# Recurrent layers: where the chosen state part is turned to features

## The chip, the cores and the metric

The kernel runs on one core of a Trainium2 chip, as one program. The metric is the device time of one launch in microseconds (us). The engines named here are TensorE (PE in the profile, with its weight loads as PEld), VectorE (DVE), ScalarE (ACT), GpSimd (POOL) and the sync engine (SP), which issues the weight loads from HBM.

## The reference, cut to what matters

Four layers run over 4 samples of 512 tokens and 512 features: an attention with shared keys, a decoder layer with two attentions and an MLP, and two recurrent layers (`L2` and `L3`). The change lies in the recurrent layers only. What they compute there, for 32 heads of 16 features each:

```
r, k, v = xr @ Wr.T, xk @ Wk.T, xv @ Wv.T            # 32 heads of 16
w = exp(-exp(decay + tanh(xw @ td_w1) @ td_w2))
def step(s, (r_t, k_t, v_t, w_t)):
    a = k_t[..., :, None] * v_t[..., None, :]
    out = einsum('bhi,bhij->bhj', r_t, u * a + s)
    return a + w_t[..., :, None] * s, out
og = (out - mean) / sqrt(var + 1e-5)                 # mean and var over the 16 of a head
x1 = x + (og * gn_w + gn_b) * g @ Wo.T
```

## The kernel before, in words

One loop (`nc.Fori`) goes over the 4 samples; a sample passes through all four layers before the next one begins. Each engine has its own instruction stream, written out by hand; semaphores join them. There is no planner: the order of the calls in the source is the order on the engine.

The features of a recurrent layer are split into `C = 4` groups of 128 (8 heads), counted by `hg`. The scan over tokens is not done step by step. Tokens are cut into blocks of 8. Inside a block, the outputs come from sums over pairs of tokens at distances that double (`pair_sums` of level 0, 1, 2 and `pair_sums4`, `bonus_low`, `bonus_high`), and these are built up in one bank of PSUM in feature-by-token layout, `y_bank`. What a token takes from the state with which its block began comes by another way. `fresh_state` makes each block's new state (128 matmuls of 32x32), DVE scans the states over the blocks (`states`), and `from_state` multiplies them with `r` (128 matmuls of 32x32) into the banks 0 to 3 of PSUM. Each of those holds four candidates, of which ACT and DVE choose one for every token by a mask: ACT in one instruction (`y_tokens`, line 1416), DVE in three (`own_block`, line 1250). The result is `y_tok`, in token-by-feature layout. `tokens_to_y` (line 990 to 994) turns it to features with 16 small products against the identity, which show as 32 matmuls in the trace, and adds it to `y_bank`. After that, ACT takes the bank out twice (`y_out`: its square to `sqT`, a copy to `yT`), and PE makes the variance of each head (`variance`).

`middle(hg, n)` gives PE other work in between: the projection of `k`, `r` or `v` for the next group (line 369, eight matmuls of 128x512 in the trace), and in the last group the gate in their place. `values_to_tokens` (line 909) turns `v` to tokens; it waits for ACT's copy `vT` (line 1375), and ACT's `value_blocks` (line 1432) spreads its result. `keys_to_tokens` (line 953) does the same for `k`, and ACT's copy of it is `k_tok` (line 1451), for which `fresh_state` waits. `pair_sums(hg, 0)` writes into bank 0, so for `hg > 0` it waits until DVE is done with `y_tok` of the group before (line 915). ACT's own order in a group is: `value_blocks`, (in the last group a copy of a weight block, line 324), `middle(hg, 0)`, `y_out(hg - 1)`, `k_tok`, then the rest.

The weights come in blocks of 1 MB into a ring of three places, `wring` (line 278). SP issues the next block as soon as the last product with the oldest one is done. In the recurrent groups that falls after the last projection of `k`, of `r` and of `v`, all in the group `hg = 2`.

The three places between two groups are called the first (`hg` 0 to 1), the middle (1 to 2) and the third transition (2 to 3). There are 8 of each: 2 layers in 4 samples.

Of the kernel before, what the change touches and what calls it, by code (L numbers as in the profile page):

```python
# [21 lines left out]
C = H // P  # L22
# [73 lines left out]
def build(nc, a, known, samples=B):  # L96
# [116 lines left out]
    with ExitStack() as stack:  # L213
# [97 lines left out]
        def w_parts(name):  # L311
            buf, k = SPLIT[name]
            return buf[:, k % 2, 0, :], buf[:, k % 2, 1, :]
# [17 lines left out]
        def parts_wait(pe, name):  # L331
            pe.wait_ge(*act_done.when('whi', name))
            pe.wait_ge(*low_made(name))
# [6 lines left out]
        def three(w, src):  # L340

            return ((w[0], src[0]), (w[1], src[0]), (w[0], src[1]))
# [486 lines left out]
        def pe_rwkv(pe, l):  # L829
# [31 lines left out]
            def project(hg, name, fcs=range(C)):  # L861
                if hg == 0 and 0 in fcs:
                    w_wait(pe, f'{name}_{l}')
                tile = take(pe, f'{name}p', l, hg) if hg > 0 else ps[:, FIRST[name], :]
                to_T(pe, tile, weights(f'{name}_{l}'), mix[:, MIX_AT[name]], hg, fcs=fcs,
                     fin=tile_ready.reach(f'{name}p', l, hg) if C - 1 in fcs else None,
                     ready=(lambda fc: mix_wait(pe, l, name, fc)) if hg == 0 else None)
# [31 lines left out]
            def gate(c):  # L899
                if c == 0:  # L900
                    w_wait(pe, f'g_{l}')
                to_T(pe, take(pe, 'gp', l, c), weights(f'g_{l}'), mix[:, MIX_AT['g']], c, fin=tile_ready.reach('gp', l, c),
                     ready=(lambda fc: mix_wait(pe, l, 'g', fc)) if c == 0 else None)

            def values_to_tokens(hg):
                pe.wait_ge(*act_emptied.when('vp', l, hg))
                tile = take(pe, 'vt', l, hg)
                for tc in range(C):
                    m = nc.tensor.matmul(tile[:, tc * P:(tc + 1) * P], vT[:, hg % 2, tc * P:(tc + 1) * P], centre[:, :],
                                         start=True, stop=True)  # L910
                m.then_inc(*tile_ready.reach('vt', l, hg))

            def pair_sums(hg, level):
                if level == 0 and hg > 0:
                    pe.wait_ge(*dve_done.when('y_tok', l, hg - 1, 3))
                pe.wait_ge(*dve_done.when('rk', l, hg, level))
                bank, src = ((0, rk0[:, :]), (1, rk1[:, :]), (2, rk2[:, :, :, :]))[level]
                nc.tensor.matmul(ps[:, bank, 0:256 if level == 1 else 512], head_sum[:, :], src, start=True, stop=True)\  # L918
                    .then_inc(*tile_ready.reach('sums', l, hg, level))

            def pair_sums4(hg):
                pe.wait_ge(*dve_done.when('rk', l, hg, 4))
                for part in range(2):
                    nc.tensor.matmul(take(pe, 'sums4', l, hg, part), head_sum[:, :], rk4[:, 2 * part:2 * part + 2, :, :],  # L924
                                     start=True, stop=True).then_inc(*tile_ready.reach('sums4', l, hg, part))
# [23 lines left out]
            def keys_to_tokens(hg):  # L949
                pe.wait_ge(*dve_done.when('k8', l, hg))  # L950
                tile = take(pe, 'kt', l, hg)
                for tc in range(C):
                    m = nc.tensor.transpose(tile[:, tc * P:(tc + 1) * P], kT[:, hg % 2, tc * P:(tc + 1) * P], ident[:, :])
                m.then_inc(*tile_ready.reach('kt', l, hg))

            def fresh_state(hg):
                for level in range(3):
                    pe.wait_ge(*dve_emptied.when('sums', l, hg, level))
                pe.wait_ge(*act_emptied.when('vt', l, hg))
                pe.wait_ge(*act_emptied.when('kt', l, hg))  # L960
                for tc in range(C):
                    for r in range(4):
                        rows_ = slice(32 * r, 32 * r + 32)
                        for q in range(4):
                            out = ps[32 * q:32 * q + 32, r, :].rearrange('p (two t x) -> p two t x', two=2, t=C)[:, :, tc, :]
                            m = nc.tensor.matmul(out, k_tok[rows_, tc, 32 * q:32 * q + 32],
                                                 v_blocks[rows_, tc, q, :, :, :].rearrange('p two b j -> p two (b j)'),
                                                 start=True, stop=True)
                m.then_inc(*S['fresh_ready'].reach(l, hg))
# [19 lines left out]
            def tokens_to_y(hg):  # L989
                pe.wait_ge(*dve_done.when('y_tok', l, hg, 3))  # L990
                for tc in range(C):
                    for p in range(4):
                        m = nc.tensor.matmul(y_bank[32 * p:32 * p + 32, tc * P:(tc + 1) * P], y_tok[:, p, tc, :], ident[:, :],
                                             start=False, stop=(tc == C - 1), skip_group_check=True)
                m.then_inc(*S['context_ready'].reach('y', l, hg))

            def variance(hg):
                pe.wait_ge(*act_done.when('sqT', l, hg))
                tile = take(pe, 'var', l, hg)
                for tc in range(C):  # L1000
                    m = nc.tensor.matmul(tile[:, tc * HEADS:(tc + 1) * HEADS], sqT[:, tc * P:(tc + 1) * P],
                                         masks[:, 4:4 + HEADS], start=True, stop=True)
                m.then_inc(*tile_ready.reach('var', l, hg))

            def roots_to_features(hg):
                pe.wait_ge(*(dve_done if hg == C - 1 else pool_done).when('rstd_j', l, hg))
                tile = take(pe, 'rs', l, hg)
                for tc in range(C):
                    m = nc.tensor.transpose(tile[:, tc * P:(tc + 1) * P],
                                            rstd_j[:, tc, :, :].rearrange('p h j -> p (h j)'), ident[:, :])  # L1010
                m.then_inc(*tile_ready.reach('rs', l, hg))

            def wo(fc, tiles=range(C)):
                if fc == 0 and 0 in tiles:
                    parts_wait(pe, f'o_{l}')
                    pe.wait_ge(*dve_done.when('y_tok', l, C - 1, 3))
                pe.wait_ge(*dve_done.when('gated_lo', l, fc))
                for tc in tiles:
                    for k, (w, x_) in enumerate(three(w_parts(f'o_{l}'), (act_hi[:, 2], act_lo[:, 2]))):
                        m = nc.tensor.matmul(ps[:, tc, :], x_[:, fc, tc * P:(tc + 1) * P], w[:, fc * H:(fc + 1) * H],  # L1020
                                             start=(fc == 0 and k == 0), stop=(fc == C - 1 and k == 2), skip_group_check=True)
                    if fc == C - 1:
                        m.then_inc(*tile_ready.reach('wo', l, tc))

            def middle(hg, n):
                if hg + 1 < C:
                    project(hg + 1, 'krv'[n])
                else:
                    gate(n)

            for hg in range(C):
                values_to_tokens(hg)
                pair_sums(hg, 0)
                pair_sums(hg, 1)
                middle(hg, 0)
                if hg > 0:
                    tokens_to_y(hg - 1)
                pair_sums(hg, 2)
                keys_to_tokens(hg)
                if hg > 0:  # L1040
                    variance(hg - 1)
                fresh_state(hg)
                pair_sums4(hg)
                bonus_low(hg)
                middle(hg, 1)
                if hg == C - 1:
                    gate(C - 1)
                if hg > 0:
                    roots_to_features(hg - 1)
                bonus_high(hg)  # L1050
                from_state(hg)
                middle(hg, 2)
            wo(0, (0, 1))
            tokens_to_y(C - 1)
            wo(0, (2, 3))
# [524 lines left out]
        with nc.Fori(0, samples) as b:  # L1580
# [8 lines left out]
            with nc.Block() as block:  # L1589
                @block.tensor  # L1590
                def _(pe):
# [32 lines left out]
                    for l in (2, 3):  # L1624
                        pe_rwkv(pe, l)
# [276 lines left out]
```

## Time and profile before

| what | us |
|---|---|
| median of 3 runs | 4186.95 |
| lowest and highest | 4186.92, 4193.72 |
| profiled execution, its own time | 4188.31 |
| its span | 4186.5 |
| PE busy | 3719.4 (89%) |
| DVE busy | 2621.0 (63%) |
| ACT busy | 2154.2 (51%) |
| POOL busy | 1652.4 (39%) |

The span reaches from the first to the last instruction that was profiled. A time in a row of the trace counts from the span's start. Busy times of engines overlap, so they don't add up to the span. The mean granted clock of TensorE in the profiled execution is 0.952 of full speed.

### The profile page before, as it was taken

What the parts mean: (1) busy time and instruction counts of PE and PEld (TensorE: products, weight loads), DVE (VectorE), ACT (ScalarE), POOL (GpSimd) and SP (SyncE); (2) the same over time, 40 slices, a digit from 0 to 9 for tenths busy, and PEclk for the clock granted to TensorE, in tenths of its full rate; (3) what the DMA queues carried; (4) which work ended last, traced back from release to release, by engine and by line L of the source; (5) the groups of instructions that cost most, each with busy time, mean ns of one, the idle gap of its engine ahead of it and who ended that gap; (6) DMA issues with size and microseconds to landing.
All of it is one profiled execution on the core that took longest, in us unless ns stands there. A gap on an engine that the chain in (4) does not pass through costs nothing. (4 is left out here: it accounts for less than half of the span.)

```text
span 4186.5 us, 66406 instructions
## 1 busy us (share of the span) xinstructions
PE 3719.4 (89%) x24448; PEld 2267.5 (54%) x24448; DVE 2621.0 (63%) x5691; ACT 2154.2 (51%) x4272; POOL 1652.4 (39%) x1849
## 2 busy tenths in 40 slices
PE   7988899899888989989888888998988888899898
PEld 4544565546554456554655445656465454565555
DVE  5765746666576564665657656467666765645766
ACT  5655733434666573343466657334346665733433
POOL 4554442232454454223245445422324544542232
PEclk9999999999999999999999999999999999999999
DMA  4032221102204122110220412211022032221102
GB/s 137 15 103 67 78 78 40 62 21 101 76 15 123 49 84 70 39 64 21 101 76 15 121 53 82 70 42 60 22 101 78 20 117 55 78 70 42 60 32 101
DMA packets 94558, 276.11 MB, mean 66 GB/s; under 512 B 25472, under 2 KB 25984, under 8 KB 73088
## 3 DMA queue, kind: packets, MB, share of 16 engines
q1 hardware_dynamic: 94208, 271.58, 20.2%
q8 instruction: 202, 3.31, 0.3%
q14 instruction: 148, 1.21, 0.1%
HBM read 201.24 MB, written 4.19 MB: 49 GB/s over the span
## 5 line engine op out<-in xcount | busy, mean ns | idle before, releaser
L805 POOL TENSOR_SCALAR probs<-probs,row_inv 128x512 f32<-128x512 f32 x1024 | 696.0, 696 | 635.1 <-DVE row_inv L720 635.1
L664 ACT ACTIVATE probs<-probs,row_max 128x512 f32<-128x512 f32 x1024 | 733.4, 725 | 132.1 <-DVE row_max L736 131.2
L559 PE MATMUL ps<-ident,probs 128*128 128x128 f32 x4096 | 606.5, 289 | 172.9 <-ACT pT L658 146.5
L559 PEld LDWEIGHTS ps<-ident,probs 128*128 128x128 f32 x4096 | 477.0, 146 | 383.0 <-ACT pT L658 211.4
L658 ACT ACTIVATE pT<-ps 128x512 f32<-128x512 f32 x768 | 430.1, 602 | 107.2 <-PE ps L559 106.5
L369 PE MATMUL ps<-mix,wring 128*128 128x512 f32 x1024 | 471.0, 596 | 3.8 <-DMA wring<-in_blocks_dram 3.8
L534 PE MATMUL ps<-kstack,qstack 96*128 96x512 f32 (+1 forms) x1024 | 380.5, 467 | 16.2 <-DMA qstack<-hi 7.1
L736 DVE CUSTOM_DVE_ANT_0 probs<-ps,maskA 128x512 f32<-128x512 f32 x512 | 329.3, 681 | 42.6 <-PE ps L534 42.6
L736 DVE CUSTOM_DVE_ANT_0 probs<-ps,neg 128x512 f32<-128x512 f32 x512 | 340.6, 685 | 8.9
L369 PEld LDWEIGHTS ps<-mix,wring 128*128 128x128 f32 x1024 | 191.2, 190 | 198.9 <-issue 178.8
L1535 POOL TENSOR_TENSOR hinv<-hvar,minus_half 128x32 f32<-128x32 f32 x24 | 146.3, 6094 | 376.8 <-DVE hvar L1255 376.8
L550 PE MATMUL ps<-pT,v 128*32 128x512 f32 x2048 | 244.6, 599 | 0.0
L369 PE MATMUL ps<-srcT,wring 128*128 128x512 f32 x512 | 238.5, 609 | 0.2
L534 PEld LDWEIGHTS ps<-kstack,qstack 96*128 96x128 f32 (+1 forms) x1024 | 177.1, 194 | 108.4 <-issue 44.1
L409 POOL TENSOR_SCALAR varep<-moments 128x1 f32<-128x1 f32 x128 | 43.0, 336 | 482.1 <-DVE moments L388 481.1
L329 POOL TENSOR_TENSOR mlp_w<-wring,mlp_w 128x2048 fp32r<-128x2048 f32 x32 | 149.5, 4672 | 194.2 <-ACT mlp_w L324 194.2
L421 PE MATMUL ps<-ident,xn 128*128 128x128 f32 x448 | 104.8, 389 | 126.6 <-DVE xn L392 126.1
L750 DVE COPY pT<-ps 128x512 f32<-128x512 f32 x256 | 168.2, 686 | 73.2 <-PE ps L559 71.7
L664 ACT ACTIVATION_READ_ACCUMULATOR probs<-probs,row_max 128x1 f32 x1024 | 205.4, 201 | 0.0
L1689 DVE TENSOR_TENSOR hidden_lo<-hidden,hidden_hi 128x512 fp32r<-128x512 f32 x64 | 94.2, 1495 | 168.7 <-ACT hidden_hi L1656 168.7
L1510 POOL TENSOR_TENSOR mix<-mix,xa 128x512 f32<-128x512 f32 x104 | 118.6, 1160 | 171.6 <-DVE mix L1126 122.4
L743 DVE TENSOR_TENSOR ps<-ps,maskA 128x1024 f32<-128x1024 f32 x128 | 156.5, 1223 | 23.1 <-PE ps L534 22.9
(177 smaller groups left out, 7025.9 us busy)
## 6 DMA issues: line engine op xcount, KB each, us to landing
wring<-in_blocks_dram SPq DMA_DIRECT2D x151, 1024.0 KB, 5.1
qstack<-hi SPq DMA_DIRECT2D x256, 64.0 KB, 2.0
kstack<-hi SPq DMA_DIRECT2D x256, 64.0 KB, 2.0
maskA<-in_mask_dram SPq DMA_DIRECT2D x9, 1024.0 KB, 7.8
rows<-in_rows_dram SPq DMA_DIRECT2D x8, 1024.0 KB, 4.6
qstack<-hi SPq DMA_DIRECT2D x256, 32.0 KB, 2.0
qstack<-lo SPq DMA_DIRECT2D x128, 64.0 KB, 2.0
kstack<-lo SPq DMA_DIRECT2D x128, 64.0 KB, 2.0
```

What stands on the lines that cost most here:

```text
L329: nc.gpsimd.tensor_tensor(low, weights(name), high.bitcast(F32), ALU.subtract).then_inc(*pool_done.reach('wlo', name))
L369: m = nc.tensor.matmul(tile, w[:, base_ + fc * H + oc * P:base_ + fc * H + (oc + 1) * P], src[:, fc, :], start=(fc == 0), stop=(fc == C - 1))
L534: nc.tensor.matmul(ps[:, qc, :], qstack[0:A.kt, g % 2, i, qc * P:(qc + 1) * P], kstack[0:A.kt, g % 2, 0 if A.shared else i, :], start=True ...
L550: ins = nc.tensor.matmul(ps[32 * h:32 * h + 32, OBANK, :], lhs, pT[:, h, kc, :], start=(kc == 0 and first), stop=(kc == C - 1 and final))
L559: ins = nc.tensor.transpose(tile[:, qc * P:(qc + 1) * P], probs[:, m % PSLOTS, qc, kc * P:(kc + 1) * P], ident[:, :])
L658: nc.scalar.activation(pT[:, m % 4, kc, :], ps[:, ring.bank('pT', t, m, kc), :], ACT.Copy)\
L664: nc.scalar.activation(p, p, ACT.Exp, bias=row_max[:, n % PSLOTS, qc:qc + 1], scale=-1.0, accum_out=row_sum[:, n % PSLOTS, qc:qc + 1]).the ...
L736: nc.vector.tensor_tensor_reduce(out=probs[:, s, qc, :], in0=ps[:, qc, :], in1=other, scale=-1.0, scalar=3.0e38, op0=ALU.add, op1=ALU.min, ...
L743: nc.vector.tensor_tensor(ps[:, two, :], ps[:, two, :], A.mask[:, two, :], ALU.mult)\
L750: nc.vector.tensor_copy(pT[:, m % 4, kc, :], ps[:, ring.bank('pT', t, m, kc), :])\
L805: nc.gpsimd.tensor_scalar(p, p, row_inv[:, (n - 1) % PSLOTS, qc:qc + 1], 1.0, ALU.mult, ALU.mult)\
L1535: nc.gpsimd.tensor_tensor(hinv[:, :, :], hvar[:, :, :], minus_half[:, :].rearrange('p (a b) -> p a b', b=HEADS), ALU.pow).then_inc(*pool_d ...
```

## The change: the step is moved by one place

PE's list of calls changes, and nothing else: the function, its waits, and the streams of the other engines stay as they are. `tokens_to_y(hg - 1)` stood in group `hg` behind the projection `middle(hg, 0)`. Now `tokens_to_y(hg)` stands at the end of group `hg`, behind `middle(hg, 2)`, for `hg` 0, 1 and 2. The call for the last group stays where it was, between two parts of `wo`.

```
                 pair_sums(hg, 0)
                 pair_sums(hg, 1)
                 middle(hg, 0)
-                if hg > 0:
-                    tokens_to_y(hg - 1)
                 pair_sums(hg, 2)
                 keys_to_tokens(hg)
                 if hg > 0:
...
                 bonus_high(hg)
                 from_state(hg)
                 middle(hg, 2)
+                if hg < C - 1:
+                    tokens_to_y(hg)
             wo(0, (0, 1))
             tokens_to_y(C - 1)
```

So PE's order across a transition was: `v` projection, `values_to_tokens`, `pair_sums` 0 and 1, `k` projection (or the gate), `tokens_to_y`, `pair_sums` 2, `keys_to_tokens`, `variance`, `fresh_state`. It becomes: `v` projection, `tokens_to_y`, `values_to_tokens`, `pair_sums` 0 and 1, `k` projection (or the gate), `pair_sums` 2, and on as before.

## Rows read from the trace of the kernel before

**Rows 1.** The profile page, busy time (us, share, instructions) and DMA queues (packets, MB, share).

```profile
PE 3719.4 (89%) x24448; PEld 2267.5 (54%) x24448; DVE 2621.0 (63%) x5691; ACT 2154.2 (51%) x4272; POOL 1652.4 (39%) x1849
...
q8 instruction: 202, 3.31, 0.3%
```

**Rows 2.** Timeline around the middle transition of sample 1, layer 2 (start, duration, instructions).

```profile
696.30 3.70 PE L369 MATMUL ps<-mix,wring 128*128 128x512 f32 x8
...
697.13 2.32 DVE L1250 SCALAR_TENSOR_TENSOR y_tok<-ps,masks,y_tok 128x512 f32<-128x512 f32 x3 [2.64 <-ACT y_tok L1416]
...
700.69 1.16 PE L909 MATMUL ps<-centre,vT 128*128 128x128 f32 x8 [0.69 <-ACT vT L1375]
...
702.97 3.60 PE L369 MATMUL ps<-mix,wring 128*128 128x512 f32 x8
...
706.50 1.08 PE L993 MATMUL ps<-ident,y_tok 128*32 128x128 f32 x32
706.60 0.33 SPq L278 DMA_DIRECT2D wring<-in_blocks_dram  x1
706.61 0.60 ACT L1375 ACTIVATE kT<-ps 128x512 f32<-128x512 f32 x1 [2.30 <-PE ps L369]
707.51 1.12 PE L918 MATMUL ps<-rk,head_sum 128*128 128x512 f32 x2
707.65 0.60 ACT L1423 ACTIVATE sqT<-ps 128x512 f32<-128x512 f32 x1 [0.44 <-PE ps L993]
708.14 0.59 ACT L1424 ACTIVATE yT<-ps 128x512 f32<-128x512 f32 x1
...
709.11 0.60 ACT L1451 ACTIVATE k_tok<-ps 128x512 f32<-128x512 f32 x1 [0.37 <-PE ps L953]
...
709.85 1.72 PE L966 MATMUL ps<-v_blocks,k_tok 32*32 32x128 f32 x108
...
713.50 0.47 PE L966 MATMUL ps<-v_blocks,k_tok 32*32 32x128 f32 x20 [1.93 <-issue]
```

**Rows 3.** Stretches, first transition (window length, each engine's busy time, PEclk, DMA share, GB/s).

```profile
667.43:694.45 27.02, 26.25 (x362) 15.86 (x363) 17.66 (x41) 8.85 (x13) 6.32 (x4) 1.00 0.01 2
```

**Rows 4.** Stretches, middle transition: two of eight, and the sum of eight.

```profile
1738.71:1770.52 31.81, 29.20 (x362) 16.87 (x362) 17.62 (x42) 8.74 (x13) 6.28 (x4) 0.89 0.14 41
...
4052.45:4079.46 27.01, 26.25 (x362) 15.86 (x362) 17.68 (x42) 8.85 (x13) 6.25 (x4) 1.00 0.17 52
sum 242.46, PE 223.61 PEld 131.28 DVE 140.89 ACT 70.56 POOL 50.04; mean PE 27.95 PEld 16.41 DVE 17.61 ACT 8.82 POOL 6.25
```

**Rows 5.** DMA queues, first transition, 675 to 677 us (packets, MB, share).

```profile
q8 instruction: 1, 0.02, 4.2%
```

**Rows 6.** DMA queues, 704 to 710.5 us: the only queue; the issue (us to landing).

```profile
q1 hardware_dynamic: 117, 0.96, 41.7%
...
wring<-in_blocks_dram SPq DMA_DIRECT2D x1, 1024.0 KB, 4.7
```

**Rows 7.** DMA queues, middle transition, 710.5 to 712 us.

```profile
q8 instruction: 1, 0.02, 5.4%
```

**Rows 8.** Timeline around the third transition of sample 1, layer 2.

```profile
737.06 0.59 ACT L1423 ACTIVATE sqT<-ps 128x512 f32<-128x512 f32 x1
...
737.90 0.69 DVE L1211 TENSOR_TENSOR rk<-ps,vT 128x512 f32<-128x512 f32 x1 [2.85 <-PE ps L918]
...
738.26 0.60 ACT L1451 ACTIVATE k_tok<-ps 128x512 f32<-128x512 f32 x1
...
742.35 0.41 PE L966 MATMUL ps<-v_blocks,k_tok 32*32 32x128 f32 x4 [1.49 <-issue]
```

**Rows 9.** Stretches, third transition: two of eight, and the sum of eight.

```profile
723.60:757.49 33.89, 31.71 (x372) 18.07 (x371) 20.57 (x44) 12.49 (x17) 8.05 (x3) 0.95 0.16 57
...
2814.93:2845.24 30.31, 29.62 (x372) 17.33 (x371) 20.76 (x43) 12.49 (x17) 10.17 (x2) 1.00 0.17 64
...
sum 268.19, PE 251.18 PEld 143.70 DVE 164.72 ACT 99.89 POOL 66.44; mean PE 31.40 PEld 17.96 DVE 20.59 ACT 12.49 POOL 8.31
```

More of the change, by code:

```diff
@@ L1035, in pe_rwkv @@
                 middle(hg, 0)
-                if hg > 0:
-                    tokens_to_y(hg - 1)
                 pair_sums(hg, 2)
@@ L1052, in pe_rwkv @@
                 middle(hg, 2)
+                if hg < C - 1:
+                    tokens_to_y(hg)
             wo(0, (0, 1))
```

## The prediction, made before the changed kernel was timed

> **What bounds the kernel now.** First the page: TensorE is busy for 89% of the span [rows 1]. So the question at each transition between two groups is what PE does and where it stands idle, and the views to read are the timeline there and the stretches from one `from_state` to the next. I give places in the middle transition of sample 1, layer 2 [rows 2]; the other 23 look alike where I don't say otherwise.
>
> PE finishes the `v` projection a little before 700.0, stands idle for 0.69 us until ACT's `vT`, starts `values_to_tokens` at 700.69, the `k` projection at 702.97, `tokens_to_y` at 706.50, `pair_sums` 2 at 707.51, and `fresh_state` at 709.82 to 709.85, right behind ACT's `k_tok`, which ends at 709.11 + 0.60 = 709.71. The reader is to see two things there: the idle 0.69 us, while DVE has finished `y_tok` at 697.13 + 2.32 = 699.45; and that `fresh_state` breaks off after 108 of its 128 matmuls and stands still for 1.93 us, for nothing that a semaphore explains ("issue").
>
> Then the stretches. A first transition takes 27.02 us [rows 3]. The eight middle ones take 242.46 us together, 30.3 on average, but the last of them takes 27.01 with the same instructions [rows 4]. So 242.46 - 8 x 27.01 = 26.4 us are lost in seven of them. PE's busy time makes 223.61 - 8 x 26.25 = 13.6 of that: the same matmuls at a lower granted clock (0.89 in the slowest, against 1.00). The other 12.8 are idle time, 1.8 in each of seven. In the third transition seven of eight have such a stop too, with 4 matmuls left [rows 8]: 268.19 - 8 x 30.31 = 25.7 us over the one that has none [rows 9], of which PE's busy time makes 251.18 - 8 x 29.62 = 14.2 and idle time 11.5.
>
> **What the stop is.** Queue 8 moved 202 packets of instructions, 3.31 MB [rows 1]. Over them, PE's 48,896 loads and matmuls make 242 a packet, so this is PE's code, coming in blocks of some 250 instructions. The stops fit the ends of blocks: a group issues 725 loads and matmuls [rows 3] and about ten waits, and the stop of the third transition is 16 matmuls (32 instructions) later in `fresh_state` than that of the middle one; together some 767, three blocks. Count one block back from the middle stop: 216 instructions of `fresh_state`, 16 of `variance`, 8 of `keys_to_tokens`, 4 of `pair_sums` 2 make 244, so the block before ends inside the last few instructions of `tokens_to_y`. When PE's sequencer comes to that point, the next block is asked for. In the first transition, where the point is 32 instructions earlier, its packet runs between 675 and 677 us [rows 5], four us before its own `tokens_to_y`: the sequencer is ahead of the array. In the middle transition no instruction packet runs from 704 to 710.5; SP's load of 1 MB, issued at 706.60 when the `k` projection frees its place, takes 4.7 us to land [rows 6], and the packet comes only behind it, between 710.5 and 712 [rows 7]. `fresh_state` uses up its block at 711.6 and waits until 713.50.
>
> The Trainium skill says, in "Runtime: NRT & Kernel Launch", section "Instruction fetch mechanics", that each engine fetches its code in blocks of 16 KiB, ahead of need, and that the cost of crossing a block is mostly hidden. The trace agrees on the size (3.31 MB over 202 packets) and not on the cost, if my reading of the stops is right. By the page's rule there would be nothing to gain from moving a block's end, and the sum would hold the order alone: that is the first rival below.
>
> **The change, part by part.** It removes and adds no instruction. It moves 64 loads and matmuls and one wait.
>
> (a) *Order on PE.* `tokens_to_y` costs 707.51 - 706.50 = 1.01 us, and 0.09 more for the change of shape before it (the projection's eight slots of 0.43 us from 702.97 end at 706.41), 1.10 in all. In its new place it starts at 699.83 (696.30 + 8 x 0.43 + 0.09), 0.38 after `y_tok` is done, so the wait that it brings costs nothing; queued behind it are only `values_to_tokens` and what follows, and these would have waited for `vT` until 700.69. They now start at 699.83 + 1.01 = 700.84: 0.15 late. So `pair_sums` 2 comes 1.10 - 0.15 = 0.95 earlier. What is late next is ACT: `kT` at 706.61 + 0.15, `sqT` and `yT`, which no longer wait for `tokens_to_y`, and `k_tok` follow at 0.49 each (708.14 - 707.65), so `k_tok` starts at 708.23 in place of 709.11. I take 0.88 us for the first and middle transitions: 16 x 0.88 = 14.1. Bounds: 0 if another chain holds `fresh_state`, 16 x 0.95 = 15.2. The chain behind `fresh_state` (sums, DVE's scan, `pairs`, `from_state`) hangs on it and comes along. In the third transition ACT is the bound already: `sqT` starts at 737.06 with no idle time before it, so it moves 0.15 later, and `k_tok` to 737.06 + 0.15 + 0.98 = 738.19 against 738.26 [rows 8]. I take 8 x 0.07 = 0.6.
>
> SP's queue: the `k` block's load is issued 0.15 later. The wait of `pair_sums(hg, 0)` for `y_tok` is met already. `y_bank` is written 5.7 us earlier; nobody reads or writes it between.
>
> (b) *The middle stop.* The count of instructions up to `fresh_state` is what it was, so the stop's place in `fresh_state` stays. But the block before it now ends in the `k` projection, since the 64 instructions of `tokens_to_y` are no longer between. The sequencer gets there some 4 us earlier than before. The packet then runs between about 701 and 705.5, ahead of the load, whose issue is at 706.75, and the block is there when `fresh_state` needs it at 710.7. I take all of the 26.4. Bounds: 0 and 26.4; the row it is nearest to is the middle transition at 27.01 us [rows 4].
>
> (c) *The third stop.* Here the block before ends in `variance`, behind the moved step, in both orders. I take it that the sequencer is held there by `fresh_state`'s first wait, for DVE's product with `pair_sums` 2, which starts at 737.90 after 2.85 us of waiting [rows 8]. That product comes 0.95 earlier with `pair_sums` 2; `fresh_state` starts only 0.07 earlier. So a stop of 1.5 becomes one of 0.6: 7 x 0.88 = 6.2. What remains is as short as the 0.69 us before `values_to_tokens`, after which the clock doesn't fall; but the clock's answer to it no row shows, and I take half of the 14.2. Bounds: 0 and 25.7. Value: 13.3.
>
> **Sum.** 14.1 + 0.6 + 26.4 + 13.3 = 54.4 us. Against the profiled execution's own 4188.3 (span 4186.5 and 1.8 around it) that gives 4133.9. The median of the runs is 1.4 lower, so I predict 4132.5, rounded to 4133.
>
> **The rivals.**
> 1. *The order alone.* Blocks are not what stops PE, or the block is asked for only when PE itself is at its end. Then, with the end among the last of the `k` projection's instructions (about 706.5), the packet still meets the load of 706.75. For it: in the middle and third transition the packet did come late, and only the first shows it well ahead. Against: that first one, and the transition at 27.01. Time: 4187 - 14.7 = 4172. Chance 0.20.
> 2. *Both stops go.* One third transition in eight has none at 30.31 us, with the same code. If 0.95 us are enough to tip the others: 4187 - 14.7 - 26.4 - 25.7 = 4120. Chance 0.11.
> 3. *Slower: the clock falls at the new seam.* `from_state`, then eight matmuls, then 32 narrow ones with 32 columns of weights: if TensorE's granted clock (2.4 GHz) went to its lower level (1.2 GHz) there in each of the 24 transitions, as it does after the stops, each would pay 29.20 - 26.25 = 2.95 us [rows 4], 70.8 in all, where 13.6 + 14.2 = 27.8 are paid now. With the order's 14.7 and the idle 12.8 gained, that is 15.5 slower: 4202. It decides from about 19 falls on. Against: the same narrow matmuls stand ahead of `fresh_state` now, and the clock is 1.00 in the first transition [rows 3]; and PE gets less idle time, not more. Chance 0.07.
> 4. *Nothing.* `k_tok` or DVE's chain holds `fresh_state` where it is, and the stops stay: 4187. The rows speak against both halves at once. Chance 0.04.
>
> **How the numbers follow.** My forecast has 0.58. Its own range, from (c) at nothing to (c) nearly whole, is 4122 to 4146. Leaving out rivals 3 and 4 and the upper edge of rival 1, the range is 4114 to 4174. A difference of less than 0.2% (8.4 us, so above 4178.6 and below 4195.3) could not be told from none. Faster by more than that: 0.58 + 0.20 + 0.11 = 0.89. Within it: 0.04. Slower: 0.07.
>
> **What would show it right or wrong.** In the new profile: `tokens_to_y` directly behind the `v` projection, with no idle time before `values_to_tokens`; the first transition at 26.1 us; the middle ones at 26.1 too, with all 128 matmuls of `fresh_state` in one piece, a clock of 1.00, and the instruction packet ahead of SP's load. If the middle ones stay near 30, (b) is wrong. The third ones at 30.2 to 33.8 tell of (c): the stop with 4 matmuls left should be about 0.6 us. If `y_tok` is what `tokens_to_y` waits for, (a) is wrong.

## The result and the profile after

The changed kernel takes 4168.6 us (median of 19 runs, 4148.0 to 4193.5), against 4186.9 beside it (19 runs, 4177.2 to 4199.9): a ratio of 0.996, interval (95%) 0.9948 to 0.9972. That is 18 us faster, where 54 were forecast. The profiled execution took 4193.5 (span 4191.6) and so lies at the upper end of its own kernel's runs. Two more executions of the same kernel, profiled later and described under the experiments, are nearer to the median. I show the order of the work from the first and take sizes from all of them.

The page after: the same instructions and the same number of code packets.

```profile
PE 3721.5 (89%) x24448; PEld 2264.1 (54%) x24448; DVE 2621.2 (63%) x5691; ACT 2149.2 (51%) x4272; POOL 1650.0 (39%) x1849
...
q8 instruction: 202, 3.31, 0.3%
```

The timeline around the middle transition of sample 1, layer 2, which answers to [rows 2] (start, duration, instructions):

```profile
703.14 3.70 PE L369 MATMUL ps<-mix,wring 128*128 128x512 f32 x8
...
703.97 2.32 DVE L1250 SCALAR_TENSOR_TENSOR y_tok<-ps,masks,y_tok 128x512 f32<-128x512 f32 x3 [3.37 <-ACT y_tok L1416]
...
706.77 1.08 PE L993 MATMUL ps<-ident,y_tok 128*32 128x128 f32 x32
...
706.88 0.60 ACT L1375 ACTIVATE vT<-ps 128x512 f32<-128x512 f32 x1 [2.94 <-PE ps L369]
...
707.78 1.16 PE L909 MATMUL ps<-centre,vT 128*128 128x128 f32 x8
...
710.07 3.60 PE L369 MATMUL ps<-mix,wring 128*128 128x512 f32 x8
...
713.50 1.02 PE L918 MATMUL ps<-rk,head_sum 128*128 128x512 f32 x2
713.70 0.33 SPq L278 DMA_DIRECT2D wring<-in_blocks_dram  x1
...
715.15 0.62 ACT L1451 ACTIVATE k_tok<-ps 128x512 f32<-128x512 f32 x1
...
715.91 1.89 PE L966 MATMUL ps<-v_blocks,k_tok 32*32 32x128 f32 x128
```

`tokens_to_y` (L993) stands behind the `v` projection, `values_to_tokens` (L909) follows with no idle time, and here `fresh_state` (L966) runs its 128 matmuls in one piece. But in sample 2 the same transition has a stop, with 20 matmuls left as in [rows 2], and longer: 2.71 us, where it was 1.93.

```profile
1750.65 0.33 SPq L278 DMA_DIRECT2D wring<-in_blocks_dram  x1
...
1752.87 1.73 PE L966 MATMUL ps<-v_blocks,k_tok 32*32 32x128 f32 x108
...
1757.30 0.70 PE L966 MATMUL ps<-v_blocks,k_tok 32*32 32x128 f32 x20 [2.71 <-issue]
```

And the first transition, which never had a stop before [rows 3], has one in three of eight. This is sample 1:

```profile
684.58 1.44 PE L966 MATMUL ps<-v_blocks,k_tok 32*32 32x128 f32 x92
687.86 1.29 PE L966 MATMUL ps<-v_blocks,k_tok 32*32 32x128 f32 x36 [1.84 <-issue]
```

The stretches from one `from_state` to the next (window, length, each engine's busy time, granted clock, DMA share, GB/s) show what such a stop costs. The first two rows and the first sum are first transitions, the next two and their sum middle ones, the last three third ones:

```profile
669.96:701.31 31.35, 29.47 (x362) 17.19 (x363) 17.57 (x41) 8.52 (x13) 6.34 (x4) 0.89 0.01 2
...
891.67:917.89 26.22, 26.14 (x362) 15.97 (x363) 17.63 (x41) 8.63 (x13) 6.32 (x4) 1.00 0.01 2
...
sum 222.73, PE 216.38 PEld 130.22 DVE 140.88 ACT 68.86 POOL 50.62; mean PE 27.05 PEld 16.28 DVE 17.61 ACT 8.61 POOL 6.33
...
701.31:727.48 26.17, 26.15 (x363) 15.92 (x362) 17.60 (x41) 8.63 (x13) 6.21 (x3) 1.00 0.16 53
...
1738.24:1769.92 31.68, 28.92 (x363) 16.98 (x363) 17.63 (x42) 8.53 (x13) 6.28 (x4) 0.89 0.13 43
...
sum 240.67, PE 224.15 PEld 132.91 DVE 140.92 ACT 68.64 POOL 49.93; mean PE 28.02 PEld 16.61 DVE 17.62 ACT 8.58 POOL 6.24
...
727.48:757.83 30.35, 29.62 (x370) 17.49 (x370) 20.78 (x44) 12.37 (x17) 10.23 (x3) 1.00 0.17 62
...
1769.92:1801.80 31.88, 31.18 (x371) 18.11 (x371) 20.89 (x43) 12.38 (x17) 8.13 (x2) 0.95 0.16 59
...
sum 267.61, PE 254.68 PEld 146.18 DVE 165.00 ACT 99.03 POOL 66.53; mean PE 31.84 PEld 18.27 DVE 20.62 ACT 12.38 POOL 8.32
```

An undisturbed transition is as long as was worked out: 26.2 for 27.0. What was not foreseen is how many are disturbed. With a stop, the two disturbed ones shown take 5.1 and 5.5 us more (31.35 - 26.22, 31.68 - 26.17), idle time and lower clock together; over the nine of this trace it is 3.8 to 6.1. The three sums make 731.0 us, against 726.8 in the trace of before (middle 242.5 [rows 4], third 268.2 [rows 9], and the eight first transitions below), and all the rest of the span is the same (3460.6 and 3459.7). So the whole difference between these two traces lies in the 24 stretches.

```profile
sum 216.12, PE 209.97 PEld 126.87 DVE 141.22 ACT 70.81 POOL 50.41; mean PE 26.25 PEld 15.86 DVE 17.65 ACT 8.85 POOL 6.30
```

### The profile page after: what moved, and what is told of

It reads as the page before. It is cut to its first block and busy times, and to the rows that moved or that the text cites. A ratio compares the mean times of both kernels' runs of the same rounds, so it can differ in the third digit from the quotient of the medians.

```text
span 4191.6 us, 66406 instructions
## 1 busy us (share of the span) xinstructions
PE 3721.5 (89%) x24448; PEld 2264.1 (54%) x24448; DVE 2621.2 (63%) x5691; ACT 2149.2 (51%) x4272; POOL 1650.0 (39%) x1849
```

## The experiments

The question was why the stops did not go. Three ideas: the stops are late blocks of PE's code, and what decides is on which instruction a block ends; they come from SP's load running in front of the packet; or they belong to `fresh_state`, whatever the blocks do. The direct test is to move the ends of all blocks and nothing else.

**Blocks moved by 72 instructions, in both kernels.** Ahead of layer 2's recurrent part PE gets 18 small products whose result is overwritten before anything reads it. Each makes two loads and two matmuls, so all that follows in that sample's layers 2 and 3 lies 72 instructions further on in its block:

```
     def pe_rwkv(pe, l):
+        if l == 2:
+            for _ in range(18):
+                nc.tensor.matmul(ps[0:32, OBANK, 0:8], ident[0:32, 0:32],
+                                 masks[0:32, 0:8], start=True, stop=True)
         pe_norm_turn(pe, f'a{l}', xn2)
```

> The changed kernel with 18 small products of 32x32 (72 loads and matmuls) put into PE's stream once per sample, ahead of the first recurrent layer; nothing else differs, so every later instruction of the recurrent layers lies 72 instructions later against the ends of the code blocks. Theory 1 (the stops are late code blocks, and only the place of a block's end decides): in layer 2 the ends fall at instruction 112, 145 and 177 of fresh_state in the three later groups, with the end before them at least 79 instructions ahead of fresh_state. No stop is left: first and middle transitions 26.1 to 26.2 us, third 30.2 us, clock 1.00 in all, total 4123 us. Theory 2 (the stops belong to the code or to the weight load, wherever the block ends): stops stay after 104 to 124 matmuls, total about 4169 us.

> The kernel before with the same 72 added loads and matmuls. Theory 1: no stops; first and middle transitions 27.0 us, third 30.3, total 4136 us. The difference from the changed kernel with the same addition is then the order alone: 8 x (0.88 + 0.88 + 0.07) = 14.7 us. Theory 2: stops stay, 4187 us.

Measured: the changed kernel 4137.0 (5 runs, 4131.7 to 4139.2), ratio 0.988 (0.9862 to 0.9898); the kernel before 4147.6 (5 runs, 4143.2 to 4149.0), ratio 0.9906 (0.9889 to 0.9923); the kernel before beside them 4188.4 (23 runs). `fresh_state` runs in one piece in all of the 48 transitions. The sums, with the products in the changed kernel (first, middle, two third transitions, third):

```profile
sum 214.54, PE 210.82 PEld 128.55 DVE 140.90 ACT 69.04 POOL 50.28; mean PE 26.35 PEld 16.07 DVE 17.61 ACT 8.63 POOL 6.29
...
sum 209.64, PE 209.17 PEld 127.77 DVE 141.17 ACT 69.03 POOL 49.98; mean PE 26.15 PEld 15.97 DVE 17.65 ACT 8.63 POOL 6.25
...
722.40:754.41 32.01, 31.28 (x370) 18.14 (x370) 20.93 (x44) 12.37 (x17) 8.01 (x3) 0.95 0.15 59
...
942.44:972.79 30.35, 29.62 (x370) 17.49 (x370) 20.77 (x43) 12.37 (x17) 10.20 (x2) 1.00 0.17 62
...
sum 247.84, PE 241.99 PEld 141.81 DVE 166.97 ACT 98.95 POOL 73.06; mean PE 30.25 PEld 17.73 DVE 20.87 ACT 12.37 POOL 9.13
```

and in the kernel before (first, middle, third):

```profile
sum 221.15, PE 211.79 PEld 127.63 DVE 141.13 ACT 70.77 POOL 50.30; mean PE 26.47 PEld 15.95 DVE 17.64 ACT 8.85 POOL 6.29
...
sum 216.03, PE 210.01 PEld 126.89 DVE 141.32 ACT 70.76 POOL 49.91; mean PE 26.25 PEld 15.86 DVE 17.67 ACT 8.85 POOL 6.24
...
sum 242.64, PE 236.89 PEld 139.04 DVE 166.31 ACT 99.86 POOL 81.62; mean PE 29.61 PEld 17.38 DVE 20.79 ACT 12.48 POOL 10.20
```

What follows: added work makes both kernels faster, by 41 us (before) and 32 (changed). The stops hang on the place of the blocks, and `fresh_state` and SP's load alone don't make them. The order is worth 216.03 - 209.64 = 6.4 us in eight middle transitions, 0.80 each. It has a price that I hadn't seen: in the new order three third transitions took 32.0 at a clock of 0.95 with no stop at all, in the old order all eight took 30.3.

Both kernels stayed 12 to 14 us above the times that were expected. In either of them four of the eight first transitions, all in layer 3, have a stop of another kind: PE stands still for 0.5 to 1.1 us inside the `v` projection that opens them, where the addition has put the end of another block. The clock stays whole after it, but first transitions take 221.2 in the kernel before for 216.1, and outside the 24 stretches it has 8 us more than without the addition.

**SP's load put behind the `r` projection,** to take it away from the middle packet. The `k` block's place in the weight ring is given back one projection later, so that two loads run together after `r`; computed is the same.

```
-    f'k_{l}': ('kp', l, 3),
+    f'k_{l}': ('rp', l, 3),
```

> The kernel before, but SP issues the load that follows the last k projection only after the last r projection, some 15 us later (one entry of the table of last uses). Theory A (the 1 MB load holds back the code block in the middle transition): the middle transitions come to 27.0 us, the third ones stay at 33.9, total 4161 us. Theory B (the block is late by itself, the load only lies behind it): the middle stops stay, total 4187 us.

> The changed kernel with the same later load. Theory A: the middle transitions, of which six in eight have a stop of 2.7 us with the packet right behind the load, come to 26.2 us; first ones keep their occasional stop; total about 4140 us. Theory B: the packet comes about 1 us after fresh_state begins, as in the first transition, and the stop shrinks from 2.7 to at most 1.9 us; total 4160 us.

Measured: before with the late load 4177.3 (12 runs, 4162.3 to 4192.0), ratio 0.9983 (0.9966 to 1.0); changed with the late load 4181.0 (12 runs, 4177.3 to 4197.0), 0.9987 (0.9973 to 1.0). In the kernel before, four of seven middle stops go (middle sum 228.6 for 242.5). They are layer 2's; layer 3 keeps the three that it had. Here is one of these, sample 2, layer 3 (timeline of PE), and the one code packet of PE from 1977 to 1979 us, when no other queue moves anything:

```profile
1976.21 1.71 PE L966 MATMUL ps<-v_blocks,k_tok 32*32 32x128 f32 x106
1979.83 0.48 PE L966 MATMUL ps<-v_blocks,k_tok 32*32 32x128 f32 x22 [1.91 <-issue]
```

```profile
q8 instruction: 1, 0.02, 3.7%
```

From 1970 to 1977 queue 8 is silent. So the packet begins 1.0 us after `fresh_state`, with no load in its way, and a stop of 1.91 follows. In the changed kernel the first transitions, which have no load either, keep three stops; the middle ones have four; the third ones get worse, with eight of eight disturbed and a sum of 277.2. What follows: a load isn't needed for a late packet. It changes how late they are, and in the kernel before perhaps how many (three for seven, by one trace each; in the changed kernel four, where its three traces with the load have six, two and one): with the load of the changed kernel, issued 2.2 us ahead of `fresh_state`, the late packet comes about 2.1 us after `fresh_state` begins and the stop is 2.7 us; without it, 1.0 and 1.9. That is also what makes the middle stop of [rows 2] and the one of 2.71 differ: in the kernel before the load is issued 3.2 us ahead, and the packets begin 0.4 to 1.6 after. None of the four expected totals came: 4177 lies between 4161 and 4187, and 4181 above both 4140 and 4160, for the third transitions got worse.

**Blocks moved by 232, by 32, by 64, and the third transition in its old order.** The next four ask three things: can a stop be put into the first transition of the old order, where there never was one (58 products ahead of `pe_norm_turn`, 232 instructions); how near must a block's end lie (8 products, 32 instructions); and what does the new order do in the third transition by itself. For that, `tokens_to_y` of the last pair of groups stays where it was:

```
     middle(hg, 0)
+    if hg == C - 1:
+        tokens_to_y(hg - 1)
     pair_sums(hg, 2)
...
     middle(hg, 2)
-    if hg < C - 1:
+    if hg < C - 2:
         tokens_to_y(hg)
```

This stands in two kernels, with `range(18)` and `range(16)` for the added products.

> The kernel before with 58 added products (232 loads and matmuls): the blocks' ends move 24 instructions the other way. In layer 2 they lie 48 instructions ahead of fresh_state in the first transition, 15 in the middle one, and in the third one inside fresh_state at 17, with none behind it there. Theory 1 (place decides): the stops change their transition. Third ones have none, 30.3 us in all eight; middle ones behave like the third ones of before (a stop of about 1.5 us near the end of fresh_state in most, 29 to 31 us); first ones, which never had a stop in this order, get some (27.0 to 31 us). Theory 2 (the stop belongs to the transition): first 27.0, middle 30.3, third 33.9 us as before.

> The changed kernel with 8 added products (32 loads and matmuls). Block ends lie 104, 71 and 39 instructions ahead of fresh_state in the first, middle and third transition of layer 2, 5 more in layer 3. Theory 1: every place behaves as it did in the transition where it lay before. First: no stop, 26.2. Middle (71, now with the weight load behind it): mostly no stop, as in the first transition of the changed kernel, some late. Third (39, with no load near): a stop in about half. Total about 4145 us. Theory 2 (order and load decide, not the place): as the changed kernel, 4169 us.

> Changed kernel with the 72 added loads and matmuls, and the third transition in the old order (tokens_to_y behind the gate's first product); only the first and middle transitions keep the new order. In the changed kernel with the addition, three of eight third transitions took 32.0 us with a clock of 0.95 and no stop, the others 30.36. Theory 1 (the new order costs clock in the third transition, where ScalarE holds fresh_state and PE stands idle ahead of variance): all eight third transitions at 30.33 us, middle ones 26.2, total 4132 us, 5 under the 4137 of the full new order. Theory 2 (that clock loss has nothing to do with the order): some third transitions stay at 32, total 4137 us.

> The same with 16 added products (64 loads and matmuls) in place of 18. In the kernels with 72, the first transitions were 0.1 to 1.4 us longer than 26.2 or 27.0, since a block ends in the first instructions of from_state and the next one just behind it. With 64 that end lies 8 instructions later. Theory 1: first transitions 26.2 us in all eight, total 4127 us, unless the block's end 71 instructions ahead of fresh_state in the third transition brings stops of 1.5 us and more there (then some third ones at 32 to 34). Theory 2 (the place of blocks is not the cause of these 0.1 to 1.4 us): 4132 us.

Measured, beside 4188.4 (7 runs):
- 232 in the kernel before: 4184.1 in one run. The third transitions are all free of stops, the middle ones have eight of eight, and the first ones have three. A disturbed first transition, and the sums of middle and third:

```profile
1712.84:1743.42 30.58, 28.16 (x362) 16.43 (x362) 17.56 (x41) 8.86 (x13) 6.31 (x4) 0.94 0.01 2
...
sum 244.66, PE 225.74 PEld 132.18 DVE 140.86 ACT 70.41 POOL 50.08; mean PE 28.22 PEld 16.52 DVE 17.61 ACT 8.80 POOL 6.26
...
sum 242.50, PE 237.00 PEld 138.78 DVE 166.18 ACT 99.88 POOL 81.48; mean PE 29.62 PEld 17.35 DVE 20.77 ACT 12.49 POOL 10.18
```

- 32 in the changed kernel: 4154.9 (4 runs, 4149.0 to 4161.9), ratio 0.9914 (0.9884 to 0.9944). The first have none, the middle two and the third six stops, where about four were expected.
- 72, third in its old order: 4132.5 (4 runs, 4128.2 to 4134.0), ratio 0.9862 (0.9833 to 0.989).
- 64, third in its old order: 4129.2 (4 runs, 4124.0 to 4134.8), ratio 0.9861 (0.983 to 0.9891). Its sums of first and third:

```profile
sum 210.57, PE 210.02 PEld 128.34 DVE 141.03 ACT 69.09 POOL 50.24; mean PE 26.25 PEld 16.04 DVE 17.63 ACT 8.64 POOL 6.28
...
sum 242.61, PE 236.85 PEld 139.03 DVE 166.35 ACT 99.88 POOL 81.63; mean PE 29.61 PEld 17.38 DVE 20.79 ACT 12.48 POOL 10.20
```

The place at which `fresh_state` breaks off moves as well, and by just what was added. These are a middle and a third transition of the changed kernel with 32, and a middle one of the kernel before with 232 (timeline of PE; `fresh_state` stands on line 969 there):

```profile
716.25 1.04 PE L969 MATMUL ps<-v_blocks,k_tok 32*32 32x128 f32 x36 [3.03 <-issue]
...
747.22 0.70 PE L969 MATMUL ps<-v_blocks,k_tok 32*32 32x128 f32 x20 [1.81 <-issue]
...
717.70 0.42 PE L969 MATMUL ps<-v_blocks,k_tok 32*32 32x128 f32 x8 [1.57 <-issue]
```

With 32 the stops leave 36 matmuls where they left 20, and 20 where they left 4: 16 matmuls and their loads, which are the 32 instructions. With 232, which is 24 short of a block, they leave 8 in place of 20.

What follows: stops go where the block ends are sent, in either order, so they are tied to the ends of blocks and not to a place in `fresh_state`. The third transition gains nothing from the new order and in the old one its clock stays whole (30.33 each, eight of eight). With 72 the first transitions of all three kernels still lose up to 1.4 us at their start, by the stops in the `v` projection; with 64 these are gone, and at most 0.3 is left. This last kernel has the lowest time of the study, 59 us under the kernel before and 39 under the changed one; its four runs overlap with those of the kernel with 72, so between these two the times don't decide.

**The changed kernel again, twice, and with the third transition alone in its old order.** The last three ask how much one execution differs from the next, and whether the first transition's stops belong to layer 2 alone. The third kernel has the edit above and no added products.

> The changed kernel once more, unedited, for a second trace: its profiled execution (4193.5 us) lay at the upper end of its runs (4148 to 4193, median 4169), so its count of stops is not typical. If the number of late code blocks is what spreads the runs, this trace's total less 4188.3 equals the difference of the 24 transitions' sum from the 726.8 us of before, to about 5 us, and at a total near 4169 the first or the middle transitions hold fewer stops than 3 and 6 in eight. If the spread comes from elsewhere, the transitions' sum does not follow the total.

> A third trace of the changed kernel, for the same: a count of stops in each transition over three traces. The first transitions' stops should again be in layer 2 alone, where the block ends 72 instructions ahead of fresh_state at the start of values_to_tokens, and not in layer 3, where it ends 77 ahead.

> The changed kernel with the third transition in the old order and no added products. Theory 1 (each transition by itself): first and middle as in the changed kernel (26.2 us, with stops in some), third as in the kernel before (33.9 us in seven of eight): total within 5 us of the changed kernel's 4169. Theory 2 (the third transition's new order gains or loses by itself, through shorter stops or through the clock): 5 to 15 us away from it, up if the shorter stop weighs more, down if the clock does.

Measured: 4169.3 and 4165.9 (spans 4167.5 and 4164.1), one run each; third in old order 4168.4 (12 runs, 4154.2 to 4185.3), ratio 0.9958 (0.9943 to 0.9973), the same as the change within what can be told. The kernel before stood at 4190.1 beside them (17 runs). The sums of first, middle and third transitions in the first repetition:

```profile
sum 219.20, PE 214.62 PEld 129.78 DVE 140.91 ACT 68.97 POOL 50.43; mean PE 26.83 PEld 16.22 DVE 17.61 ACT 8.62 POOL 6.30
...
sum 219.66, PE 213.67 PEld 129.22 DVE 141.02 ACT 68.97 POOL 49.89; mean PE 26.71 PEld 16.15 DVE 17.63 ACT 8.62 POOL 6.24
...
sum 264.52, PE 252.35 PEld 145.56 DVE 165.87 ACT 99.01 POOL 66.51; mean PE 31.54 PEld 18.19 DVE 20.73 ACT 12.38 POOL 8.31
```

and in the second:

```profile
sum 227.75, PE 219.86 PEld 131.57 DVE 140.78 ACT 68.69 POOL 50.55; mean PE 27.48 PEld 16.45 DVE 17.60 ACT 8.59 POOL 6.32
...
sum 214.60, PE 211.65 PEld 128.48 DVE 141.00 ACT 68.99 POOL 49.85; mean PE 26.46 PEld 16.06 DVE 17.62 ACT 8.62 POOL 6.23
...
sum 265.39, PE 252.82 PEld 145.76 DVE 165.57 ACT 98.97 POOL 66.61; mean PE 31.60 PEld 18.22 DVE 20.70 ACT 12.37 POOL 8.33
```

The number of stops over 1 us in `fresh_state`, in eight transitions of each kind, and how far the end of the block before lies ahead of `fresh_state` (in loads and matmuls of layer 2; layer 3 has 5 more). The distances are counted back by one block from where the stops break `fresh_state` off, with the added instructions put on top, so they are good to a few instructions:

```
                      first        middle       third
before                0/8 (-72)    7/8 (-39)    7/8 (-7)
before, late load     0/8 (-72)    3/8 (-39)    7/8 (-7)
before + 72           0/8 (-144)   0/8 (-111)   0/8 (-79)
before + 232          3/8 (-48)    8/8 (-15)    0/8
changed               3/8 (-72)    6/8 (-39)    5/8 (-7)
changed, again        2/8          2/8          4/8
changed, again        4/8          1/8          4/8
changed, late load    3/8          4/8          8/8
third in old order    1/8          3/8          7/8
changed + 32          0/8 (-104)   2/8 (-71)    6/8 (-39)
changed + 72          0/8 (-144)   0/8 (-111)   0/8 (-79)
```

The two kernels with the third transition in its old order and 72 or 64 added have none in 48. What was expected of the first repetition held: its total is 19.0 us under 4188.3 and its 24 transitions 23.4 under 726.8, with two and two stops. What was expected of the second did not hold throughout: a first transition of layer 3 had a stop too, in the first repetition and again in the last kernel. It is rarer there, 2 of 20 against 11 of 20 in layer 2. The place doesn't decide alone, it sets a chance, and a chance that differs with the order of the work: at 71 to 77 ahead, 0 of 24 in the old order (first transitions of two traces, and the third ones with 64 added), and 13 of 40 in the new one (first transitions of five traces; 2 of 8 more in the middle transition with 32 added). From 79 on there is none in either.

## Why the prediction was wrong

The direction was right; the size was three times too large. The time is outside the 4122 to 4146 that the prediction gave to its own forecast, and inside the wide 4114 to 4174 only because that was drawn to take in the first rival too.

**(a) The order: right within 1.2 us.** 16 x 0.88 = 14.1 was forecast. Undisturbed first and middle transitions went from 27.0 [rows 3, 4] to 26.2, 0.8 each. With 72 added to both, the kernel with the new order in the first and middle transitions alone is 4147.6 - 4132.5 = 15.1 us faster, of which 12.9 lie in these 16 transitions (221.2 + 216.0 - 214.6 - 209.6). `tokens_to_y` costs its wait nothing: DVE's `y_tok` ends at 703.97 + 2.32 = 706.29 and the step starts at 706.77. The 0.6 for the third transition didn't come: 30.35 against 30.31 [rows 9].

**(b) The middle stop: the step that failed.** The prediction said that "the sequencer gets there some 4 us earlier than before", that the packet would then run ahead of the load, and took all of the 26.4. That stops are late code blocks was right, and in sample 1 it went as drawn, with the packet 6.1 us ahead of `fresh_state`. But that the block ends earlier doesn't make the packet come in time. In the thirteen traces it begins either 1.8 us or more ahead of `fresh_state` or else after this has begun, mostly by 1.0 us (2.1 with the load in its way), and the same instructions show both from one sample to the next; two packets lie between, at 0.06 ahead and 0.09 after. Nor does the load alone make the packet of [rows 7] late, as the prediction had it: in the kernel before with the late load, layer 2 has no late one, but layer 3 has three, 1.0 to 1.5 us after the start. By the two repetitions, whose times are the median's, the middle transitions fell by 242.5 - (219.7 + 214.6) / 2 = 25.4 in place of 33.4: 6.5 by the order, and 18.9 in place of 26.4 by stops that went. In the trace first shown only 1.8 came, none of it from stops: one fewer, and the others longer.

The same step was wrong a second time, by what it left out. It let the move act on the one block that it followed, put new stops in other transitions at nothing without giving a reason, and took the first transition as free of stops, "26.1 us", because it had been so. Its block end is now 72 instructions ahead of `fresh_state` with the `k` projection where `tokens_to_y` was, and it is late in 2 to 4 of 8. First transitions went up by (219.2 + 227.8) / 2 - 216.1 = 7.4, where the order alone gives -6.5 (8 x 0.81): a new loss of 13.9. This is the largest single part of what is missing.

**(c) The third stop: mis-sized.** 13.3 and the order's 0.6 were forecast, (264.5 + 265.4) / 2 - 268.2 = -3.2 came. The step that failed here is "a stop of 1.5 becomes one of 0.6". It rested on the sequencer being held by `fresh_state`'s first wait, for DVE's product. In the new order that product ends earlier against `fresh_state` (1.4 us ahead of it in place of 0.4), and the late packets don't come earlier: they begin 0.8 to 1.0 us after the start of `fresh_state` in the first trace, and 0.9 to 1.1 in the trace of before. This is sample 1, layer 3, of the first trace (timeline, then the code packet of PE from 966 to 967 us; from 964.14 to 966 there is none):

```profile
963.45 0.69 DVE L1211 TENSOR_TENSOR rk<-ps,vT 128x512 f32<-128x512 f32 x1 [1.91 <-PE ps L918]
...
965.55 1.84 PE L966 MATMUL ps<-v_blocks,k_tok 32*32 32x128 f32 x122
...
969.26 0.64 PE L966 MATMUL ps<-v_blocks,k_tok 32*32 32x128 f32 x6 [1.87 <-issue]
```

```profile
q8 instruction: 1, 0.02, 7.6%
```

The product is done at 964.14, and the packet comes after 966. So the stops are fewer, not shorter: the eight over 1 us of the two repetitions have a mean of 1.6 us, as the seven of before had. The idle time in these stretches fell by 4.6 us, and PE's busy time rose by 1.4 where 7.1 less was forecast. For the clock, which the prediction left half open, answers badly: stretches of 31.9 to 32.0 at 0.95 have no stop of 1 us and are 1.6 over the undisturbed one, all of it PE's busy time (31.18 - 29.62).

**The account.** Forecast 54.4; by the two repetitions 7.4 - 25.4 - 3.2 = -21.2, and the spans differ by 4186.5 - 4165.8 = 20.7. Missing are 33.2: 13.9 new stops in the first transitions, 7.5 middle stops that stayed, 10.7 in the third, 1.1 of the order. Had the blocks ended elsewhere in both kernels, the change would have brought the order's gain less the clock's loss in the third transition, and no more: 4147.6 to 4137.0 with 72 added.

**The rule on blocks.** A stretch with a stop is 3.6 to 5.5 us longer in the rows shown. In the kernel before that makes 26.4 + 25.7 = 52 us in all, 1.2% of the time, and the time fell by 41 us with 72 idle instructions. The Trainium skill, "Runtime: NRT & Kernel Launch", section "Instruction fetch mechanics", calls the cost of a crossing mostly hidden. By count it is: of the 202 packets, 14 go with a stop in the transitions before. But the trace disagrees where a block ends shortly ahead of `fresh_state`'s 256 short instructions.

**The rivals.** Rival 1, the order alone at 4172, is the nearest to the measured 4168.6, and that is luck, since its mechanism isn't what happened: stops did go in the middle, and came in the first transitions. Rival 3's clock fall exists, at another seam than it was put at (ahead of `variance` in the third transition, not the 24 new seams) and mostly at 1.6 us, not 2.95.

## What to carry to other kernels

A stop of an engine that no semaphore explains, always with the same number of instructions left, points to the code stream; then every move of instructions can shift the odds of the blocks around it, the ones that had no stop included, and the gain of a reordering can't be read until the blocks are held apart from it. Test with a few idle instructions ahead of the region, at two or three amounts; here 64 of them, with the third transition left in its old order, took off twice as much as the change did (39 us against 18). When one execution differs from the next by 1%, count the disturbed stretches in more than one trace before giving a size to anything.

## What the runs showed of the hardware

- A block's data are of use some 1.4 us after its packet ends: in [rows 7] the packet is over at about 712 and `fresh_state` goes on at 713.50. Over the 101 places in the thirteen traces where `fresh_state` breaks off, it is 1.2 to 1.6 us, median 1.4, whatever the order and the added instructions. The one packet that began 0.06 us ahead of `fresh_state` left a stop of only 0.41. This ties the stops to the packets most closely. `fresh_state` issues 216 loads and matmuls in 1.72 us [rows 2], so a packet that begins 1.0 us after its start, takes 0.9 to 1.4 and is of use 1.4 later comes too late by 1.6 to 2.1, about what the stops last.
- After a stop of 1.1 to 3.0 us TensorE's granted clock mostly falls from 2.4 to 1.2 GHz for a part of what follows: matmuls that come every 0.43 us come every 0.85. In the stretch's row that is 0.89 to 0.95 on average and up to 3.3 us of busy time (29.47 against 26.14). Of 100 stretches with a stop over 1 us, 96 show it. The four without are after stops of 1.11, 1.45, 1.51 and 1.93 us; the last is the transition of [rows 2] itself, which is 2.1 us longer than an undisturbed one and not 3 to 5:

```profile
694.45:723.60 29.15, 26.51 (x362) 15.89 (x363) 17.59 (x42) 8.85 (x13) 6.24 (x4) 1.00 0.15 45
```

- In the third transition of the new order the clock falls to the same level in some samples after an idle time of only 0.69 us, ahead of `variance`, which waits for ACT's `sqT`: of the 21 such transitions without a stop over 1 us it fell in 12, after the same 0.69. In the changed kernel, sample 1 (timeline; here the clock stayed whole, 30.35):

```profile
740.82 0.69 DVE L1211 TENSOR_TENSOR rk<-ps,vT 128x512 f32<-128x512 f32 x1 [1.90 <-PE ps L918]
...
741.84 1.06 PE L1001 MATMUL ps<-masks,sqT 128*128 128x8 f32 x8 [0.69 <-ACT sqT L1423]
...
742.15 0.62 ACT L1451 ACTIVATE k_tok<-ps 128x512 f32<-128x512 f32 x1
```

  In the old order `tokens_to_y` fills that place, and it never fell without a stop in the 24 third transitions of the kernels with 72 or 64 added. The idle 0.69 us stand ahead of `values_to_tokens` there. Why the clock answers in one place and not in the other no run shows.
- Executions of the changed kernel spread over 1.1% (4148 to 4193). In its three traces the 24 transitions take 703 to 731 us, and the rest of the span stays within 3456 to 3464: the spread is mainly the number of late blocks, though between the two repetitions the rest differs by more (8 us) than the transitions do (4).

What stays open is when PE's sequencer asks for the next block. That late packets without a load near them mostly begin 0.8 to 1.1 us after the start of `fresh_state`, wherever the block's end lies before it (7 to 72 instructions), would fit a sequencer that is held by the last wait there, for `k_tok`; no run moved that wait by itself. That a block's end 72 instructions ahead of `fresh_state` is sometimes late in the new order and never in the old, and that without the load layer 2 (39 ahead) had no middle stop and layer 3 (44 ahead) had three of four, no experiment here explains; no trace shows the asking, only the packet.
